# Removal phase of a four-layer graph kernel: the 0/1 block is added to the codes on TensorE, and two hand-overs are moved

## What is computed

```python
def _dilate_pattern(adj_bool, mask_b):
    def step(carry, n):
        row = jnp.take(carry, n, axis=0)
        nbi = row.astype(jnp.int32)
        num = jnp.sum(nbi)
        sf = jnp.where(num > T_DIL, (num + K_DIL - 1) // K_DIL, 1)
        rank = jnp.cumsum(nbi)
        rm = row & (rank % sf == 0)
        valid = (mask_b[n] != 0) & (num > 1)
        rm = jnp.where(valid, rm, False)
        keep = ~rm
        carry = carry.at[n].set(row & keep)
        carry = carry.at[:, n].set(carry[:, n] & keep)
        return (carry, None)
    out, _ = jax.lax.scan(step, adj_bool, jnp.arange(N))
    return out
```

## Time and profile before

| | before |
|---|---|
| median of 3 runs | 1387.33 us |
| profiled execution | 1389.99 us, span 1388.3 us |
| TensorE matmul busy | 1176.5 us (85%) |
| VectorE busy | 814.0 us (59%) |
| ScalarE busy | 614.8 us (44%) |
| mean granted TensorE clock | 0.924 of 2.4 GHz |
| removal phase | 163.4 to 384 us |

### The profile page before, as it was taken

How to read it: one execution, slowest core, us unless ns; L and a number is a source line. 1 busy time by engine, 2 the same in 40 slices (tenths; PEclk the granted TensorE clock), 3 DMA queues, 4 the chain that set the end, 5 groups by cost and what they waited for, 6 DMA issues and landing times. The chain is left out here.

```text
span 1388.3 us, 28432 instructions
## 1 busy us (share of the span) xinstructions
PE 1176.5 (85%) x10649; PEld 1028.9 (74%) x10649; DVE 814.0 (59%) x2816; ACT 614.8 (44%) x1510; POOL 83.1 (6%) x64
## 2 busy tenths in 40 slices
PE   4798879886488989988959999599997299998998
PEld 4798856554367777777859999599997298987554
DVE  4799577778755555565532343334454457766883
ACT  5699637766644444554222323313333223222541
POOL 2012000000000000000000000000000324310000
PEclk9899989975599999999979999799999589999999
DMA  9866000000045654456304563136675235671931
GB/s 324 284 245 243 32 2 3 2 3 2 2 182 215 240 220 188 187 200 239 123 31 166 199 242 123 44 146 228 237 296 226 85 120 223 264 275 77 409 119 46
DMA packets 75950, 225.35 MB, mean 162 GB/s; under 512 B 4960, under 2 KB 23584, under 8 KB 75808
## 3 DMA queue, kind: packets, MB, share of 16 engines
q1 hardware_dynamic: 75088, 223.40, 42.7%
q10 hardware_dynamic: 720, 0.07, 0.0%
HBM read 185.70 MB, written 37.75 MB: 161 GB/s over the span
## 5 line engine op out<-in xcount | busy, mean ns | idle before, releaser
L1332 PE MATMUL lay_acc<-lay_z,k_keepadj 128*128 128x128 f32 x1024 | 117.0, 275 | 0.0
L1332 PE MATMUL lay_acc<-lay_z,k_otheradj 128*128 128x128 f32 x1024 | 116.6, 275 | 0.0
L1332 PEld LDWEIGHTS lay_acc<-lay_z,k_keepadj 128*128 128x128 f32 x1024 | 115.6, 192 | 0.0
L1332 PEld LDWEIGHTS lay_acc<-lay_z,k_otheradj 128*128 128x128 f32 x1024 | 115.5, 192 | 0.0
L1416 DVE TENSOR_TENSOR lay_o<-lay_ring,k_vec 128x512 f32<-128x512 f32 x32 | 22.1, 692 | 135.3 <-PE lay_ring L1325 135.3
L1371 ACT ACTIVATE lay_junk<-lay_o 128x128 bf16<-128x128 f32 x128 | 37.7, 295 | 136.2 <-DVEq L1439 136.2
L1081 ACT ACTIVATE fuse_dist<-fuse_prank,k_kb 128x512 f16<-128x512 f32 (+2 forms) x96 | 55.3, 576 | 76.4 <-PE fuse_prank L974 73.0
L319 PE MATMUL att_acc<-att_rhs,att_adjT 128*128 128x130 f32 x512 | 63.2, 290 | 17.5 <-DMA att_adjT<-in_adj_cols 11.3
L319 PEld LDWEIGHTS att_acc<-att_rhs,att_adjT 128*128 128x128 f32 x512 | 62.5, 205 | 18.1 <-POOLq L276 18.1
L974 PE MATMUL fuse_prank<-k_fore,k_T 128*128 128x128 fp8e5 (+3 forms) x416 | 63.4, 291 | 11.0 <-PEq L140 7.5
L319 PE MATMUL att_acc<-att_rhs,k_keepadj 128*128 128x130 f32 x512 | 61.7, 285 | 7.9 <-DVEq L429 3.3
(11 more groups left out here) (268 smaller groups left out, 2623.2 us busy)
## 6 DMA issues: line engine op xcount, KB each, us to landing
k_keepadj<-in_adj_cols SPq DMA_DIRECT2D x28, 1024.0 KB, 8.1
k_keepadj<-keptT SPq DMA_DIRECT2D x12, 2048.0 KB, 10.5
k_otheradj<-keptT SPq DMA_DIRECT2D x12, 2048.0 KB, 11.5
att_adjT<-in_adj_cols SPq DMA_DIRECT2D x16, 1024.0 KB, 6.7
k_otheradj<-in_adj_cols SPq DMA_DIRECT2D x16, 1024.0 KB, 10.6
keptT<-k_keepadj SPq DMA_DIRECT2D x16, 1024.0 KB, 5.1
keptT<-k_otheradj SPq DMA_DIRECT2D x16, 1024.0 KB, 4.4
k_keepadj<-in_adj_cols SPq DMA_DIRECT2D x8, 2048.0 KB, 10.9
```

The lines of the kernel that those rows point to most:

```text
L1332: mm = t.matmul(acc[i % 2][k][:, ib % HB, :], adjT[i % 2][:, jb, ib * P:(ib + 1) * P], zz[i % 2][:, jb, :], start=(jb == 0), stop=(jb == N ...
```

## The change

Three edits in `removal_phase`, and one constant in `attention_phase`.

1. TensorE adds 4096 times the 0/1 block to the codes: `big8` is 4096 on the diagonal, and per graph one matmul of `big8` with the block's own rows of `T8` joins the group. ScalarE takes the sum with Identity and a bias of -4096 straight to `cand`: an entry that is 1 keeps its code, one that is 0 becomes negative and meets none of the comparisons. `later`, its conversion and VectorE's product go, with their waits.
2. The comparisons are signalled after four graphs and after eight, and TensorE's sums of `hit` go graph group by graph group, for each after its own signal.
3. The flag's reduction stands between the second and the third step of `far_parameters`.

```diff
+                v.tensor_scalar(K["big8"][:], K["ident16"][:], 4096.0, None, ALU.mult, saturate=False)
...
+                        t.matmul(o[:, e * 2 * P:e * 2 * P + wide(nb)], K["big8"][:], T8[:, b, nb, n0:n0 + wide(nb)], start=False, stop=False)
                         mm = t.matmul(o[:, e * 2 * P:e * 2 * P + P], K["low8"][:], K["minus8"][:], start=False, stop=True)
...
-                    pe.wait_ge(hits, n)
-                    for h in spans:
-                        for b in range(B):
-                            mm = add(pk[:, h, b:b + 1], hit[:, b, h * P:(h + 1) * P], K["ones16"][:, 0:1])
+                    for g in range(2):
+                        pe.wait_ge(hits, 2 * n - 1 + g)
+                        for h in spans:
+                            for b in range(4 * g, 4 * g + 4):
+                                mm = add(pk[:, h, b:b + 1], hit[:, b, h * P:(h + 1) * P], K["ones16"][:, 0:1])
...
-                    if c == 0 and nb > 0:
-                        act.wait_ge(cand_ready, 2 * nb)
-                    a.activation(code[:, 4 * c:4 * c + 4, 0:wide(nb)], o[:].rearrange("p (e k) -> p e k", e=4)[:, :, 0:wide(nb)],
-                                 ACT.Copy).then_inc(code_ready, 1)
+                    a.activation(cand[nb % 2][:, 4 * c:4 * c + 4, 0:wide(nb)], o[:].rearrange("p (e k) -> p e k", e=4)[:, :, 0:wide(nb)],
+                                 ACT.Identity, bias=minus4096[:, 0:1]).then_inc(cand_ready, 1)
...
-                        later_columns(nb + 1, 0)
...
+                v.memset(minus4096[:], -4096.0).then_inc(minus_ready, 1)
...
+                    if not flagged:
+                        dve.wait_ge(flag_sum, nb + 1)
+                        v.tensor_reduce(flag[:], pk[0:1, 2, :], AX, ALU.max)
+                        dve.drain().then_inc(flag_ready, 1)
                     dve.drain()
                     v.tensor_tensor(shift[nb % 2][:], s1, u, ALU.add)
...
-                    dve.wait_ge(later_ready, 2 * nb + h + 1)
-                    dve.wait_ge(code_ready, nb * (B // 4) + h + 1)
-                    v.tensor_tensor(cand[i][:, gs, 0:k], code[:, gs, 0:k], later[:, gs, 0:k], ALU.mult)
-                    dve.drain().then_inc(cand_ready, 1)
+                    dve.wait_ge(cand_ready, 2 * nb + h + 1)
```

More of the change, by code:

```diff
@@ L486, in removal_phase @@
     with Scope(nc, "rem") as s:
-        code = s.sb("code", [P, B, 2 * P], F16)
-        later = s.sb("later", [P, B, 2 * P], BF16)
         cand = [s.sb(f"cand{i}", [P, B, 2 * P], F16) for i in range(2)]
@@ L714, in _ @@
                 act.wait_ge(minus_ready, 1)
-                for half in range(2):
-                    later_columns(0, half)
                 norm_root(nc, act, K, row, 0)
@@ L733, in _ @@
                         codes(nb + 1, 1)
-                        later_columns(nb + 1, 1)
                     if nb > 0:
@@ L745, in _ @@
                 num, y, fh, dn, two, od, c1, base, half, kprev, u, e1, e2, s1, a1, b1, b2 = (w[:, i] for i in range(17))
-                v.memset(minus1[:], -1.0).then_inc(minus_ready, 1)
+                v.memset(minus1[:], -1.0)
+                v.memset(minus4096[:], -4096.0).then_inc(minus_ready, 1)
                 v.memset(pl[:], 0.0).then_inc(pl_clear, 1)
@@ L770, in hits, with far_parameters @@
                         last = v.tensor_scalar(hit[:, b, 0:k], cand[nb % 2][:, b, 0:k], 1.0, c1[:, b:b + 1], ALU.add, ALU.is_equal)
-                    last.then_inc(done, 1)
-                def far_parameters(nb):
+                        if b % 4 == 3:
+                            last.then_inc(done, 1)
+                def far_parameters(nb, flagged):
                     v.scalar_tensor_tensor(u, ev[:], 0.5, fh, ALU.mult, ALU.mult)
@@ L839, in _ @@
                     v.tensor_tensor(moved[:], pk[:, 0, :], kprev, ALU.not_equal).then_inc(moved_ready, 1)
-                    far_parameters(nb)
-                    dve.wait_ge(flag_sum, nb + 1)
-                    v.tensor_reduce(flag[:], pk[0:1, 2, :], AX, ALU.max)
-                    dve.drain().then_inc(flag_ready, 1)
+                    far_parameters(nb, False)
                     go = dve.value_load(flag_bits, min_val=0, max_val=FLAG_MAX)
@@ L1930, in build_program @@
             resident("low8", [P, P], F8, codes)
+            resident("big8", [P, P], F8, codes)
             resident("back8", [P, N], F8, codes)
```

12 lines of the change are left out of this document (3 added, 9 removed).

## The result

| | before | after |
|---|---|---|
| median, interleaved runs on the same chip | 1388.39 us (1386.73 to 1394.24, 6 runs) | 1381.85 us (1380.24 to 1383.61, 6 runs) |
| ratio, 95% interval | | 0.9941 (0.9926 to 0.9957) |
| profiled execution, span | 1389.99 us, 1388.3 us | 1382.0 us, 1380.3 us |
| mean granted clock | 0.924 | 0.928 |
| removal phase | 163.36 to 384.08: 220.7 us | 163.75 to 375.32: 211.6 us |

The ratio is 8.2 us of 1388.39 (6.0 to 10.3), faster by more than 0.3%; the two medians differ by 6.5 us, the spans of the two profiled executions by 8.0. The forecast of 1382.2 us lies beside the median after.

A forecast was written before the change was run, and what follows sets the result against it. The prediction took the removal phase as a relay between TensorE, ScalarE and VectorE; its terms, summed block by block as a running shift, came to -5.1 us from the median of 1387.33, giving 1382.2 us, range 1377.0 to 1388.5.

The forecast's parts named there:

- a relay: Removal phase: no single engine bounds a stage; a microsecond counts only on the engine holding the baton there.
- TensorE's matmuls: 64 added matmuls: 0.11 us per 256 columns at the upper clock; in all 6.5 us, or 12.6 at 1.2 GHz.
- ScalarE's codes with a bias: Codes' copy from PSUM with a bias: 1,111 ns, 0.09 us more than before; far bound 1,240 ns.
- The conversions: ScalarE's 16 conversions removed: in round 2, where ScalarE holds it, the first group's distances start 0.96 us earlier.
- VectorE's product: Product removed: 0.81 us saved for the second half of each block's candidates, where VectorE holds the start.
- The flag: Reduction moved earlier at block starts: TensorE gets the flag 0.48 us earlier; VectorE saves 0.16 us.
- second rival: Half of it: flag bound by TensorE's counts, dearer bias, another drain; -2.7 us left, 1384.6 us; chance 0.33.
- The halves: Comparisons signalled in halves: some 0.1 us saved where TensorE waits for them, nothing where it comes late itself.
- The opening: Before block 0, TensorE held, both groups on the path: +0.25 us; running sum +0.71 after block 0's groups.
- the clock's rival: Some 10 us of the third stage go at 2.4 GHz: 1378 to 1379 us, or 1386 by loss; chance 0.14.
- the waits for ring slots: Sign of being right: TensorE's waits for ScalarE to empty ring slots, 11.7 us, fall by 4 us.
- the fuse phase: Sign of being right: the phase behind the removal starts near 379 us instead of 384.1.

The follow-up runs named there:

- keep_conversion: The changed kernel with ScalarE's 16 conversions put back, into a tile nobody reads: 1392.72 us, ratio 1.0015 against the kernel before.
- keep_product: The changed kernel with VectorE's 16 products put back, into a tile nobody reads: 1386.16 us, ratio 0.9965 against the kernel before.
- matmul_only: The kernel before with TensorE's 64 matmuls added on a zero block and nothing taken away: 1397.6 us, ratio 1.0038.
- codes_only: The kernel before with the first edit alone (block added to codes, conversion and product gone): 1385.66 us, ratio 0.9955.
- flag_only: The kernel before with the third edit alone, the flag's reduction moved: 1390.03 us, ratio 0.9985.
- warm_opening: `warm` with twelve more filling matmuls ahead of block 0's first round: 1378.34 us, ratio 0.9918 against the kernel before.
- warm: The changed kernel with unused filling matmuls ahead of each flag and of the first rounds of blocks 5 to 7: 1379.48 us, ratio 0.9918 against before.
- warm_before: The kernel before with the same filling matmuls as `warm`: 1391.41 us, ratio 0.9999 against the kernel before.

## Why the prediction was right, and where its sum was not

- **What bounds the phase, a relay:** right. Work taken from ScalarE (`keep_conversion`) and from VectorE (`keep_product`) both cost time when put back, and so did work given to TensorE (`matmul_only`). No engine alone would show all three.
- **TensorE's matmuls:** 0.11 us for 256 columns was right at the upper clock (274.70 to 274.81 above). The sum books some 6.5 us of them as on the path (0.87 or 0.88 in each block from the opening to block 5 and half of it in block 6, less the slacks); alone they cost 5.3, and that while the time at 1.2 GHz fell by 8 us (1.8 us by the mean price), so about 7 by waiting. The edits measured singly or put back singly add up to -12.0 us (5.3 - 10.7 - 3.8 - 2.1 - 0.7), and together they give -8.2. The intervals leave some 5 to 6 us of uncertainty in that sum of five, so it is open whether they add.
- **ScalarE's codes with a bias:** 1,113 ns against 1,111; the row from PSUM was the right neighbour, and 1,240 ns was the wrong one. By the Trainium skill ("ScalarE: Activation LUTs", Rules for kernel authors) the estimate was 1.15 us, 3% over.
- **The conversions: the step that was mis-sized.** The prediction has -0.96 us for the first of a block and nothing for the second, and gives no reason for the nothing. The second stands ahead of ScalarE's copy to `T8`; TensorE's counts wait for that copy, and behind them stands the flag's read: 0.80 us at 260.86 in `keep_conversion`. With the clock the conversions are worth 10.7 us, in waiting alone some 6 to 8, and the sum's terms for them come to 4.3 to 4.9. Shown are the stalls behind the first conversion and the counts behind the second: from `moved` to the far codes it is 2.36, 2.75, 2.78, 2.43, 3.06, 2.23, 2.01 us at the starts 1 to 7 with the conversions, 2.35, 2.03, 2.02, 2.01, 2.14, 2.01, 2.01 without, 3.0 us in all, some of which VectorE may hide from start 4 on. How the whole spreads over the two was not separated.
- **VectorE's product:** right. 3.8 us (about 1 to 6.5) against 4.0 to 4.5. From `moved` to the next block's first sum it is 0.77, 0.77, 1.17 and 0.48 us less after than in `keep_product` at the starts of blocks 4 to 7, where the prediction had 0.81 three times and 0.56; against the kernel before, with VectorE's part of the flag edit, it is 0.97, 0.99, 1.36 and 0.54 less, predicted 0.97 three times and 0.72.
- **The flag:** 0.48 us predicted at TensorE, 0.49 between `codes_only` (2.52) and after (2.03), and 2.1 us alone in the medians. It rests on a condition that the prediction named only as part of its second rival: TensorE's own counts must be done. In VectorE's queue the reduction stands where it should, here with block 1's flag and the start of block 4:

```profile
230.12 0.16 DVE L773 TENSOR_TENSOR rem_w<-rem_w 128x8 f32<-128x8 f32 x1
...
230.20 0.15 DVE L776 TENSOR_REDUCE rem_flag<-rem_pk 1x1 f32<-1x8 f32 x1
...
286.06 0.17 DVE L844 COPY rem_w<-rem_pk 128x8 f32<-128x8 f32 x1 [1.38 <-issue]
...
286.14 0.41 DVE L787 TENSOR_SCALAR rem_final<-rem_cand 128x1024 bf16<-128x1024 f16 x1
```

  The reduction starts 0.08 us behind L773. But the operation behind it waits 0.17 us more, and from `moved` to the end of the row's last operation (kb after, the reduction before) it is 1.43 us against 1.49: 0.06 saved for VectorE, not 0.16. At the start of block 4 the comparison (286.14) follows the copy at once; the product of the earlier trace rows is gone.
- **The halves:** the four matmuls now start apart, the second four after a wait of 0.38 us, where before all eight came behind 0.72 us:

```profile
289.13 0.27 PE L540 MATMUL rem_pk<-k_ones,rem_hit 128*128 128x1 bf16 x4
289.78 0.27 PE L540 MATMUL rem_pk<-k_ones,rem_hit 128*128 128x1 bf16 x4 [0.38 <-DVE rem_hit L759]
```

  -0.7 us alone, with an interval that includes both 0.9 and zero. Not settled.
- **The opening:** +2.1 us for the opening and block 0 in the two profiles where +0.7 was said. What the sum lacks here is the place of the slow stretch. It ended at 171.4 us, 7.7 us behind the phase's start, before at 168.9, 5.6 behind it, so that it lay over the codes, which were priced at the upper clock. `flag_only` has the instructions of the kernel before up to this point, but its slow stretch ended 7.6 us behind the start, and it needs 31.06 us where the kernel before needs 29.62. `keep_conversion` has the new matmuls and the bias, and its slow stretch ended 5.5 us behind the start: 30.14 us, +0.5 over the kernel before. The two rows, `flag_only` first:

```profile
163.22:194.28 31.06, 24.52 (x384) 21.08 (x384) 17.28 (x98) 8.98 (x10) 0.00 (x0) 0.73 0.01 2
```

```profile
163.46:193.60 30.14, 24.99 (x400) 21.82 (x400) 15.24 (x97) 9.10 (x9) 0.00 (x0) 0.80 0.01 2
```

  So the clock's place in the opening is worth 1.4 us between two profiles of the same instructions, as much as was measured beyond the prediction's +0.7. In `warm_opening` the first slow stretch ended early too (5.1 us behind the start) and the first sum came 1.2 us earlier than in `warm`, but the next slow stretch lay a microsecond later, and at `moved` the gain was gone.
- **The clock:** the prediction gave it 0.14 as a rival of its own and set as its mark a mean clock of the phase that moves by more than 0.03. It went from 0.755 to 0.792. The mark was met just so, and by the prediction's own words the clock's rival then holds and not the sum alone. But the rival's time, 1378 to 1379, did not come: it priced a microsecond at 1.2 GHz at 0.3 to 0.4 us in a stage in which TensorE is busy three quarters of the time; the mean price of the runs is 0.22, and in block 5, which lies in that stage, next to nothing. Part of the time at 1.2 GHz went back behind the phase, where it grew from 89.4 to 97.0 us. The Trainium skill ("TensorE: Matmul & The Clock Gate", What's actually happening) calls the throttled state the default that activity releases; the blocks agree, since blocks 1 and 2, in which TensorE is busy over nine tenths, have 0.95 and 1.00, and the last stretch, where it is busy a third, has 0.50.

So the mechanism held, the sum was short, and that the forecast of 1382.2 us lies beside the measured 1381.85 is in part luck. The phase lost 4 us more than the sum: 5.4 more in blocks 1 to 7, by conversions that were under-priced and by the clock, less 1.4 in the opening. Behind the phase 0.8 us and at its start 0.4 us came back, which leaves 8.0 us between the spans where 5.1 were said. The other 2.9 us are the base: the prediction's rows come from an execution of 1389.99 us and its forecast starts from the median of three runs, 1387.33; the profiled execution after, 1382.0, lies at its median. Of the signs, the waits for ring slots fell by 4.1 us where 4 was said, but the fuse phase began at 375.3 us, not near 379.

How the 4 us divide between waits and clock stays open. The clock's mean price would alone give 4.5, and block 2 by its own price 1.3 of its 1.7. The pair at a like clock leaves 1 to 3 us over the sum for waits (6.3 us by the two profiles, 7.9 by the executions, less 5.1). With a spread between executions of up to 5 us in `warm_before` neither is exact.

## What to carry to other kernels

Before pricing an operation at nothing because nobody seems to wait for the one behind it, follow the in-order queues two hand-overs further: here ScalarE's conversion stood before a copy, the copy before TensorE's counts, and the counts before the one read that opens the block. In a relay between three engines an operation that goes from the engine holding the baton can pay more than the one wait by which it was priced, and edits that touch the same hand-over are better measured together too, since nothing here shows that their single prices add. Filling TensorE's idle time raises its clock and is cheap to try, but price a microsecond at the lower clock by its place: in the pairs seen here it was 0.4 to 0.5 us where TensorE was busy over nine tenths of the time, and next to nothing where other engines held the relay. Before reading two profiles against each other, look where the slow stretches lie in each.

## What the hardware showed that was not expected

- One program on one core, in twelve executions, took 1387.7 or 1392.8 us on the mean of two separate groups, with mean granted clocks of 0.934 and 0.925. A comparison of few executions can differ by 5 us for that reason alone.
- A microsecond at 1.2 GHz instead of 2.4 went with 0.22 us in the mean of these two groups, but with 0.39 and 0.49 us in blocks 2 and 1 and with 0.01 in block 5; and from 81.3 to 66.0 us at 1.2 GHz (`warm` to `warm_opening`) brought nothing that the ratios show (0.9918 both).
- The same instructions took 29.62 or 31.06 us in the opening and block 0, by where the slow stretch lay (it ended 5.6 or 7.6 us behind the phase's start).
- Two stalls of TensorE, 1.2 to 1.3 and 0.55 us, stood ahead of a fall of the clock in one kernel (`keep_conversion`, block 3) and of none in the rest of the block in another (before, block 3).
- More columns on TensorE made its clock higher and the kernel slower (`matmul_only`: 100.1 us at 1.2 GHz against 108.1 in one profile each, and +5.3 us).
